# Loading the stacks of q and k for one group at a time, instead of for two

## The chip, the core and the metric

The kernel runs on one core of one Trainium2 chip. The metric is the device time of one execution in microseconds (us). The core has five engines with a queue of instructions each: PE (TensorE, matmuls), DVE (VectorE), ACT (ScalarE), POOL (GpSimd) and SP (SyncE, which here only issues DMA transfers and waits). All DMA transfers share 16 DMA engines. The engines meet only through semaphores.

## The reference

Two layers over x of shape (4, 512, 512). Only the first one has to do with the change. With `xn = layernorm(x)` it is

```python
q = rope((xn @ wq).reshape(4, 512, 32, 16))      # 32 heads of 16
k = rope((xn @ wk).reshape(4, 512, 8, 16))       # 8 heads of 16, each for 4 heads of q
v = (xn @ wv).reshape(4, 512, 8, 16)
...
attn = softmax(q @ k.T / 4 + causal mask)
s = (attn @ v) @ wo
logits = xn @ W_gate + b_gate                    # top 2 of 8 experts for each token
y = relu(xn @ W_e[e] + b_e[e]), mean over the 2 experts of the token
x = x + s * silu(y)
```

The second layer is a long convolution of the layer norm of x, times the silu of a linear layer.

## The kernel before

There are three stages. Stage A (to about 100 us) projects x to q, k, v and gate logits and turns q and k. They are written to DRAM, as two fp32r parts each (a high part and the rest), in `qk_d`, which the profile calls `turned_parts`. Stage B (about 100 to 580 us) is attention and the expert layer, woven into each other. Stage C is the second layer.

**Groups.** Stage B walks over 32 groups, 4 batches `b` times 8 heads of k, `h`; here a group's number is g = 8b + h. A group is the 4 heads of q that share one head of k. Each of its two halves (`s`) has on the partitions a stack of three pieces of 16 rows, (high, low), (high, high), (low, high), so that one matmul over 48 rows gives the product of q and k in nearly full precision. The stack of k is `kt`, that of q is `qt`. Both have four buffers, `[h // 2 % 2, h % 2]`: group g + 4 takes the buffers of group g.

**The two products.** For each group PE makes the scores twice: `scores_1` (10 pieces, L1601), from which DVE takes the maxima (L1399), and `scores_2` (10 pieces, L1627 and L1630), in which two more rows of `qt` bring in the negative maxima and which ACT exponentiates (L1522). The maxima are turned by PE (`turn_maxima`, L1640), rounded by DVE into `m_rows` (L1416, L1418), and put under `qt` by two small transfers, one issued by SP and one by ACT (`maximum_rows`, L1320). Then `values` (L1657) multiplies with v.

**The order on PE in iteration g**, with expert or output matmuls ("quarters" of a tile, L1685 and L1696) between the parts by the table `SIZES`:

```python
scores(e, (3, 4, 5, 6), following, (0, 1, 2, 3), (b, h))
quarters(b, h, 0)
scores(e, (7, 8, 9), following, (4, 5, 6), (b, h))
quarters(b, h, 1, 0, TURN_AFTER)
turn_maxima(e, *following)
quarters(b, h, 1, TURN_AFTER)
scores(e, (0, 1, 2), after, (7, 8, 9), (b, h))
```

The first tuple is of `scores_1`, of `following` (g + 1) or `after` (g + 2); the second is of `scores_2` of g itself. So iteration g needs the stack of g + 2 right behind `turn_maxima`, and is done with the stack of g itself a little later, at the end of the last line.

The number of quarters differs from group to group. From the `turn_maxima` of iteration g to the next there are mostly 8, but 5 for g = 5, 9, 13, 17, 21 and 25, then 7 for g = 6, 10, 14, 18, 22 and 28, and 6 for g = 26 and 27. A quarter is one matmul of 128 x 512 for a tile, which the profile counts as two rows.

**The queue of SP in iteration g** (`go` of `sp_b`) is written in this order: transfers for the expert tiles (`shuffles(b, h, 0)`: L1776 loads the rows of a tile into `xg`, named `arena` in the profile, L1779 stores gathered rows to `gathered_rows`), the maxima of g + 1 (L1320), stores of expert results (L1785), the stacks (odd g only: `load_stacks` for g + 3 and g + 4, L1313 for `kt` and L1314 for `qt`), more tiles (`shuffles(b, h, 1)`), stores, and a few weights. DVE turns a loaded tile (`expert_x`, L1464) before PE can multiply it. SP, DVE and PE all take their instructions strictly in order.

`load_stacks` waits on `b_s2`, the count of pieces of `scores_2`, until the two groups that hold the pair of buffers are through: for g + 3 and g + 4 that is the end of `scores_2` of g. Stacks 0 to 3 are loaded ahead of the loop, and the q and k of group 0 once more, earlier, by `load_first` into `qt_first`.

Of the kernel before, what the change touches and what calls it, by code (L numbers as in the profile page):

```python
# [33 lines left out]
R = H // KV  # L34
# [130 lines left out]
def due(n):  # L165


    return not isinstance(n, int) or n > 0
# [49 lines left out]
def build(nc, x_d, wq_d, wk_d, wv_d, wo_d, wg_d, bg_d, we_d, be_d, lam_d, p_d, q_d, vct_d, ct_d, bp_d, dd_d,  # L218
          step_d, wft_d, sc_d, bf_d, const_d, dft_d, out_d):
    ctx = ExitStack()  # L220
    with ctx:
# [9 lines left out]
        def sems(name, n):  # L231
            return [sem(f"{name}{i}") for i in range(n)]
# [200 lines left out]
        def sp_a(e):  # L433
# [22 lines left out]
            for b in range(NB):  # L456
                for u in range(TPB):
# [2 lines left out]
                        store_parts(e, b - 1, u - 2)  # L460
                    if (b, u) == (NB - 2, 0):
                        load_first(e)
            load_stacks(e, 0, 0)

        def dve_a(e, st):
            v = nc.vector
# [766 lines left out]

        b_init = sem("b_init")
        b_first = sem("b_first")
        b_ld = sems("b_ld", 2)
        b_wo = sem("b_wo")
        b_v = sem("b_v")
        b_tm, b_me, b_mr = sem("b_tm"), sem("b_me"), sem("b_mr")
# [19 lines left out]
        def nth_of(per, b, h, k):  # L1259

            return b * (NG * per) + (h * per + k)
# [26 lines left out]
                    e.dma_start(kt[at:at + HD, 0].bitcast(F32), k_rows[of_k]).then_inc(b_first, 16)  # L1288
                    e.dma_start(qt_first[at:at + HD].bitcast(F32).rearrange("i r t -> i (r t)"), q_rows[of_q, s]).then_inc(b_first, 16)

        def load_stacks(e, b, h):

            e.wait_ge(b_init, 4)
            for half in range(2):
                e.wait_ge(a_ps[half], 16 * (b + 1))
            if due(at := nth_of(NJ, b, h, -2 * NJ)):
                e.wait_ge(b_s2, at)
            if not due(b) and h == 0:
                for par in range(2):
                    e.wait_ge(a_xn[par], NT // 2)  # L1300
            if not due(b) and h == 2:
                for u in (2, 3):
                    e.wait_ge(a_store[u], 16 * NB)
                for par in range(2):
                    e.wait_ge(a_kvg[par], NT // 2)
            buf = h // 2 % 2
            q_rows = qk_d[b][:, R * HD * h:R * HD * (h + 2), :].rearrange("c (g s i r) t -> c s i g (r t)", g=2, s=2, r=HALF)
            k_rows = qk_d[b][:, D + HD * h:D + HD * (h + 2), :].rearrange("c (g i) t -> c i g t", g=2)
            for s in range(2):
                for piece, (of_q, of_k) in enumerate(((0, 0), (0, 1), (1, 0))):  # L1310
                    at = 64 * s + HD * piece
                    if (b, h) != (0, 0):
                        e.dma_start(kt[at:at + HD, buf].bitcast(F32), k_rows[of_k]).then_inc(b_ld[buf], 16)  # L1313
                    e.dma_start(qt[at:at + HD, buf].bitcast(F32).rearrange("i g r t -> i g (r t)"), q_rows[of_q, s]).then_inc(b_ld[buf], 16)  # L1314

        def maximum_rows(e, b, h, s):

# [261 lines left out]
        def scores_1(e, b, h, n):  # L1579
# [4 lines left out]
            if n == 0 and alone_in_bank:  # L1584
                e.wait_ge(b_first, 16 * NLD)
            elif n == 0:
                buf = h // 2 % 2
                e.wait_ge(b_ld[buf], b * (2 * 16 * NLD) + 16 * NLD * (h // 4 + 1) - (16 * NLD // 2 if buf == 0 else 0))
            if n == 2 and b == 0 and h in (1, 2):
                e.wait_ge(b_me, h)  # L1590
            if (b, h) == (0, 1) and n == 0:
# [175 lines left out]
        def sp_b(e):  # L1767
# [19 lines left out]
            def go(b):  # L1787
                for h in range(NG):
                    shuffles(b, h, 0)
                    if b * NG + h + 1 < NB * NG:  # L1790
                        maximum_rows(e, *next_group(b, h, 1), 0)
                    stores(b, h, 0, 1)
                    if h % 2 and b * NG + h + 3 < NB * NG:
                        load_stacks(e, *next_group(b, h, 3))
                    shuffles(b, h, 1)
                    stores(b, h, 2, 3)
                    transform(b, h)
                    if (b, h) in STORES:
                        store_parts(e, NB - 1, STORES.index((b, h)))
                    if (b, h) in WEIGHTS:  # L1800
                        out_weights(WEIGHTS.index((b, h)))
# [26 lines left out]
                e.wait_ge(a_kvg[par], NT // 2)  # L1828
            for x in (E - 2, E - 1):
                load_expert(e, x)  # L1830
            load_stacks(e, 0, 2)
            for b in range(NB):
                go(b)

# [421 lines left out]
```

## Time and profile before

| | us |
|---|---|
| median of 3 runs | 687.88 (686.79 to 691.36) |
| the profiled execution | 685.05 |
| its span, first to last instruction | 683.3 |
| PE busy in it | 617.3 |
| DVE busy in it | 551.2 |

The span is 1.75 us shorter than the time of the same execution. The profiled execution is 2.83 us below the median of the runs.

### The profile page before, as it was taken

The page shows a single profiled execution, that of the slowest core. Times are in us where ns is not written, and L with a number is a line of the kernel's source. Part 1 is how long each engine was busy: PE and PEld are TensorE (multiplying, and loading weights), DVE is VectorE, ACT ScalarE, POOL GpSimd, SP SyncE. Part 2 cuts the span into 40 slices and gives each one's busy share as a digit, 9 for nine tenths or more (in the row PEclk, how much of TensorE's full clock was granted, in tenths as well). Part 3 has the DMA queues.
Part 4 walks back from the last instruction along what each step waited for, and adds up shares of the span by engine and source line. Part 5 has one row for each costly group of instructions (what it writes and reads, how often), then busy time and mean ns, then how long its engine had stood idle before and what let it go on. Part 6 is the DMA issues. An engine that isn't in the chain of part 4 may idle for free.

```text
span 683.3 us, 12195 instructions
## 1 busy us (share of the span) xinstructions
PE 617.3 (90%) x3541; PEld 351.0 (51%) x3565; DVE 551.2 (81%) x1789; ACT 285.4 (42%) x535; POOL 239.5 (35%) x364
## 2 busy tenths in 40 slices
PE   9899998988997999799799889979989899899997
PEld 5788784434443444344344434434434443378886
DVE  6698899869987679788778868977888885869995
ACT  4353325424343335334344433434444445334442
POOL 3777541423232213223221322322123113676630
PEclk9999999979998999999999989999999999999999
DMA  8599978789789365575735647584464816768841
GB/s 271 145 327 246 337 215 170 164 143 295 129 268 213 93 114 101 142 146 158 179 92 105 101 125 146 162 190 88 93 130 121 203 63 216 176 142 209 205 121 77
DMA packets 79903, 113.10 MB, mean 166 GB/s; under 512 B 9705, under 2 KB 42665, under 8 KB 79841
## 3 DMA queue, kind: packets, MB, share of 16 engines
q1 hardware_dynamic: 68098, 86.90, 50.4%
q0 software_dynamic: 6704, 18.62, 12.7%
q10 hardware_dynamic: 5038, 6.84, 4.2%
q8 instruction: 29, 0.48, 0.3%
q14 instruction: 34, 0.27, 0.2%
HBM read 72.15 MB, written 39.65 MB: 164 GB/s over the span
## 4 chain that ended last, share of the span: by engine, by line
PE 52%; DVE 16%; DMA 13%; SPq 8%; issue 5%; POOL 2%; ACT 2%; ACTq 2%; DVEq 0%; POOLq 0%
PE bank L1685 16%; PE bank L1657 8%; DMA qt<-turned_parts 7%; DVE bank L1399 6%; PE bank L2173 6%; PE bank L1601 6%; PE bank L1696 4%; PE bank L2178 4%; PE bank L1026 3%; DMA turned_parts<-qk_parts 3%; SPq L1313 3%; SPq L1314 3%; DMA w_e<-expert_rows,slots 3%; PE bank L1627 1%; DVE m_rows L1418 1%
## 5 line engine op out<-in xcount | busy, mean ns | idle before, releaser
L1399 DVE CUSTOM_DVE_ANT_0 bank<-bank,cst 128x384 f32<-128x384 f32 (+3 forms) x512 | 234.3, 523 | 68.8 <-PE bank L1601 66.6
L1522 ACT ACTIVATE arena<-bank 128x512 f32<-128x512 f32 x320 | 169.6, 601 | 181.1 <-PE bank L1627 128.2
L1337 POOL TENSOR_SCALAR_AFFINE_SELECT arena<-arena 128x512 f32<-128x512 f32 x128 | 80.8, 644 | 329.2 <-ACT arena L1522 329.2
L1685 PE MATMUL bank<-w_e,arena 128*128 x312 | 156.8, 628 | 5.3 <-issue 4.0
L1601 PE MATMUL bank<-kt,qt 48*128 48x512 f32 (+1 forms) x496 | 110.9, 340 | 33.0 <-DMA qt<-turned_parts 20.6
L1601 PEld LDWEIGHTS bank<-kt,qt 48*128 48x128 f32 x496 | 68.9, 189 | 100.9 <-DVE arena L1399 43.8
L1627 PE MATMUL bank<-qt,kt 50*128 50x512 f32 x256 | 95.1, 455 | 0.4 <-ACT arena L1522 0.4
L1685 PEld LDWEIGHTS bank<-w_e,arena 128*128 128x128 f32 x312 | 57.6, 198 | 52.1 <-issue 48.0
L1657 PE MATMUL bank<-arena 128*32 128x512 f32 (+3 forms) x1024 | 78.7, 445 | 0.0
L1399 DVE DVE_READ_ACCUMULATOR2_ANT arena<- 128x1 f32 x512 | 72.0, 141 | 0.0
L1696 PE MATMUL bank<-w_proj,arena 128*128 128x512 f32 x128 | 67.7, 654 | 0.8 <-ACT s_tok L1513 0.8
L1657 PEld LDWEIGHTS bank<-arena 128*32 128x32 f32 x1024 | 28.4, 111 | 55.3 <-issue 46.9
L1532 ACT ACTIVATE arena<-bank 128x512 f32<-128x512 f32 x39 | 23.4, 599 | 63.0 <-PE bank L1685 62.9
L1627 PEld LDWEIGHTS bank<-qt,kt 50*128 50x128 f32 x256 | 45.1, 188 | 4.2 <-ACT arena L1522 3.3
L1026 PE MATMUL bank<-proj_high,xh 128*128 128x264 f32 (+1 forms) x128 | 46.1, 360 | 0.4 <-DVE xl L526 0.4
L1026 PE MATMUL bank<-proj_low,xh 128*128 128x264 f32 (+1 forms) x128 | 43.4, 339 | 0.0
L1026 PE MATMUL bank<-proj_high,xl 128*128 128x264 f32 (+1 forms) x128 | 43.4, 339 | 0.0
L858 POOL TENSOR_TENSOR s_tok<-arena 128x256 f32<-128x256 f32 (+1 forms) x64 | 33.6, 558 | 26.1 <-DVE arena L545 20.4
L1349 POOL DMA_INDIRECT s_tok<-xn_rows,slots_i x39 | 38.8, 994 | 10.9 <-ACT arena L1522 3.8
L1696 PEld LDWEIGHTS bank<-w_proj,arena 128*128 128x128 f32 x128 | 23.0, 199 | 25.8 <-issue 21.6
L541 DVE TENSOR_TENSOR arena<-bank,cst 128x128 f32<-128x128 f32 (+1 forms) x63 | 27.1, 475 | 5.4 <-PE bank L1026 5.1
L1923 POOL DMA_INDIRECT w_e<-expert_rows,slots x16 | 27.2, 1701 | 11.3 <-DMA w_e<-expert_rows,slots 8.1
(168 smaller groups left out, 942.8 us busy)
## 6 DMA issues: line engine op xcount, KB each, us to landing
qt<-turned_parts SPq DMA_DIRECT2D x96, 128.0 KB, 5.7
turned_parts<-qk_parts SPq DMA_DIRECT2D x8, 1280.0 KB, 8.3
gathered_rows<-s_tok SPq DMA_DIRECT2D x39, 256.0 KB, 5.2
arena<-gathered_rows SPq DMA_DIRECT2D x39, 256.0 KB, 4.4
expert_rows<-arena SPq DMA_DIRECT2D x39, 256.0 KB, 2.5
w_e<-in_L_ffn_W_e ACTq DMA_DIRECT2D x24, 256.0 KB, 6.0
kt<-turned_parts SPq DMA_DIRECT2D x96, 64.0 KB, 5.4
arena<-in_L_attn_x SPq DMA_DIRECT2D x16, 256.0 KB, 6.8
```

The lines of the kernel that those rows point to most:

```text
L858: i = g.tensor_tensor(o[:, :, :, c, :], xc[:, :, :, c, :], xs[:, :, :, 1 - c, :], op)
L1026: i = t.matmul(out[u % 2][:, 0:n], x[:, u % 2, k, :], w[part][:, k, :], start=(k == 0 and x is xh and part == 0), stop=(k == KB - 1 and pa ...
L1337: g.affine_select(out=diag, in_=diag, compare_op=ALU.is_ge, fill=0.0, base=0, pattern=[[0, 2], [0, HALF], [1, P]], channel_multiplier=-1). ...
L1349: e.indirect_dma_start(xr[m % 3], None, xn_d, bass.IndirectOffsetOnAxis(ap=slots_i[:, m:m + 1], axis=0)).then_inc(m_x[m % 3], 16)
L1399: i = v.tensor_tensor_reduce(out=part, in0=part, in1=const("mask")[:, S - w:], scale=1.0, scalar=LOWEST, op0=ALU.add, op1=ALU.max, accum_o ...
L1522: nc.scalar.activation(pt[:, s, first:second + 1:second - first].rearrange("p c r q -> p c (r q)"), s2_bank(b, h, n).rearrange("p (c x) -> ...
L1601: i = t.matmul(s1_bank(b, h, n)[:, at:at + w], stack[rows, x if r is None else r, q * P:w], kt[rows, h // 2 % 2, h % 2, 0:w], start=(x == ...
L1627: i = t.matmul(to, keys(j), queries[:, q:q + 2], start=True, stop=True)
L1657: i = nc.tensor.matmul(bank[4][VW * r:VW * (r + 1), j * P:], vb[:, j, h, :], pt[:, r // HALF, at:at + TPB - j, r % HALF, :], start=(j == O ...
L1685: i = t.matmul(bank[7], xgt[:, m % 2, k * P:(k + 1) * P], w_e[:, ex[m], k, :], start=False, stop=(k == KB - 1))
L1696: i = t.matmul(bank[to], ot[:, (b * PAIRS + k) % (PAIRS + 1), u, :], wo[:, k, :], start=(k == 0), stop=(k == KB - 1))
L2173: i = t.matmul(bank[2 + u % 2][:, :], x[:, u % 2, k, :], (w_high, w_low)[part][:, k, :], start=(k + n == 0), stop=(k + n == KB + 1))
```

## The change

The stacks are loaded by `load_stack`, for one group, in twelve transfers of 16 rows (six of `kt`, 32 KB each, six of `qt`, 64 KB each). Before they were twelve for two groups, of 64 and 128 KB. The load of group g + 4 is issued in every iteration g, behind `shuffles(b, h, 1)`, and waits for the end of `scores_2` of g. There are four semaphores `b_ld` in place of two. Bytes and buffers are the same.

```diff
-        def load_stacks(e, b, h):
+        def load_stack(e, b, h):
...
-            if due(at := nth_of(NJ, b, h, -2 * NJ)):
+            if due(at := nth_of(NJ, b, h, -3 * NJ)):
                 e.wait_ge(b_s2, at)
...
-            buf = h // 2 % 2
-            q_rows = qk_d[b][:, R * HD * h:R * HD * (h + 2), :].rearrange("c (g s i r) t -> c s i g (r t)", g=2, s=2, r=HALF)
-            k_rows = qk_d[b][:, D + HD * h:D + HD * (h + 2), :].rearrange("c (g i) t -> c i g t", g=2)
+            keys, queries, loaded = kt[:, h // 2 % 2, h % 2], qt[:, h // 2 % 2, h % 2], b_ld[h % 4]
+            k_rows = qk_d[b][:, D + HD * h:D + HD * (h + 1), :]
+            q_rows = qk_d[b][:, R * HD * h:R * HD * (h + 1), :].rearrange("c (s i r) t -> c s i (r t)", s=2, r=HALF)
             for s in range(2):
                 for piece, (of_q, of_k) in enumerate(((0, 0), (0, 1), (1, 0))):
                     at = 64 * s + HD * piece
-                    if (b, h) != (0, 0):
-                        e.dma_start(kt[at:at + HD, buf].bitcast(F32), k_rows[of_k]).then_inc(b_ld[buf], 16)
-                    e.dma_start(qt[at:at + HD, buf].bitcast(F32).rearrange("i g r t -> i g (r t)"), q_rows[of_q, s]).then_inc(b_ld[buf], 16)
+                    if b or h > 1:
+                        e.dma_start(keys[at:at + HD].bitcast(F32), k_rows[of_k]).then_inc(loaded, 16)
+                    e.dma_start(queries[at:at + HD].bitcast(F32).rearrange("i r t -> i (r t)"), q_rows[of_q, s]).then_inc(loaded, 16)
...
             elif n == 0:
-                buf = h // 2 % 2
-                e.wait_ge(b_ld[buf], b * (2 * 16 * NLD) + 16 * NLD * (h // 4 + 1) - (16 * NLD // 2 if buf == 0 else 0))
+                e.wait_ge(b_ld[h % 4], 16 * NLD * (2 * b + h // 4 + 1) - (16 * NLD // 2 if h % 4 < 2 else 0))
...
                     stores(b, h, 0, 1)
-                    if h % 2 and b * NG + h + 3 < NB * NG:
-                        load_stacks(e, *next_group(b, h, 3))
                     shuffles(b, h, 1)
+                    if b * NG + h + 4 < NB * NG:
+                        load_stack(e, *next_group(b, h, 4))
                     stores(b, h, 2, 3)
```

Ahead of the loop, `load_stacks(e, 0, 0)` and `load_stacks(e, 0, 2)` become two calls of `load_stack` each.

The queue of SP in iteration 6, before, from the maxima of group 7 to those of group 8 ("..." stands for more rows of the same two kinds):

```order
L1320 DMA qt<-m_rows 2x8x128 [waits b_me]
L1785 DMA expert_rows<-arena 128x512 [waits m_ye]
L1779 DMA gathered_rows<-s_tok 128x4x128 [waits m_x1]
L1823 DMA w_proj<-in_L_attn_wo 16x4x512 x2
L1776 DMA arena<-gathered_rows 128x512 [waits m_xt,m_xs0]
L1320 DMA qt<-m_rows 2x8x128 [waits b_me]
```

The same iteration with the change:

```order
L1321 DMA qt<-m_rows 2x8x128 [waits b_me]
L1785 DMA expert_rows<-arena 128x512 [waits m_ye]
L1779 DMA gathered_rows<-s_tok 128x4x128 [waits m_x1]
L1314 DMA kt<-turned_parts 16x512 [waits a_ps1,b_s2,a_ps0,b_init]
L1315 DMA qt<-turned_parts 16x1024
...
L1823 DMA w_proj<-in_L_attn_wo 16x4x512 x2
L1776 DMA arena<-gathered_rows 128x512 [waits m_xt,m_xs0]
L1321 DMA qt<-m_rows 2x8x128 [waits b_me]
```

The load of stack 10 now stands in iteration 6, behind the tile transfer L1779 and ahead of L1823 and L1776; before, iteration 6 had no load.

The queue of SP in iteration 0, before, from the maxima of group 1 to those of group 2:

```order
L1320 DMA qt<-m_rows 2x8x128 [waits b_me]
L1779 DMA gathered_rows<-s_tok 128x4x128 [waits m_x0]
L1779 DMA gathered_rows<-s_tok 128x4x128 [waits m_x1]
L1776 DMA arena<-gathered_rows 128x512 [waits m_xs0]
L1776 DMA arena<-gathered_rows 128x512 [waits m_be,m_xs1]
L1779 DMA gathered_rows<-s_tok 128x4x128 [waits m_x2]
L1320 DMA qt<-m_rows 2x8x128 [waits b_me]
```

With the change:

```order
L1321 DMA qt<-m_rows 2x8x128 [waits b_me]
L1779 DMA gathered_rows<-s_tok 128x4x128 [waits m_x0]
L1779 DMA gathered_rows<-s_tok 128x4x128 [waits m_x1]
L1314 DMA kt<-turned_parts 16x512 [waits a_ps1,b_s2,a_ps0,b_init]
L1315 DMA qt<-turned_parts 16x1024
...
L1776 DMA arena<-gathered_rows 128x512 [waits m_xs0]
L1776 DMA arena<-gathered_rows 128x512 [waits m_be,m_xs1]
L1779 DMA gathered_rows<-s_tok 128x4x128 [waits m_x2]
L1321 DMA qt<-m_rows 2x8x128 [waits b_me]
```

The load of stack 4 moved ahead of the first two tile loads (L1776); before, stacks 4 and 5 were loaded in iteration 1, behind the second L1320.

## Rows read from the trace of the kernel before

**Rows 1.** The page, busy time: engine, us, share of the span, instructions.
```profile
PE 617.3 (90%) x3541; PEld 351.0 (51%) x3565; DVE 551.2 (81%) x1789; ACT 285.4 (42%) x535; POOL 239.5 (35%) x364
...
```

**Rows 2.** The page, the chain that ended last, by line.
```profile
PE bank L1685 16%; PE bank L1657 8%; DMA qt<-turned_parts 7%; DVE bank L1399 6%; PE bank L2173 6%; PE bank L1601 6%; PE bank L1696 4%; PE bank L2178 4%; PE bank L1026 3%; DMA turned_parts<-qk_parts 3%; SPq L1313 3%; SPq L1314 3%; DMA w_e<-expert_rows,slots 3%; PE bank L1627 1%; DVE m_rows L1418 1%
```

**Rows 3.** Waits of PE: total us, times, longest us.
```profile
PE bank L1601 <- DMA qt<-turned_parts: 20.6, 8, 4.1
```

**Rows 4.** Timeline, PE: start, us, what, [idle before it <-releaser].
```profile
217.83 0.79 PE L1601 MATMUL bank<-kt,qt 48*128 48x512 f32 x1 [3.82 <-DMA qt<-turned_parts]
...
511.85 0.50 PE L1601 MATMUL bank<-kt,qt 48*128 48x512 f32 x1 [2.17 <-DMA qt<-turned_parts]
...
537.86 0.49 PE L1601 MATMUL bank<-kt,qt 48*128 48x512 f32 x1 [1.28 <-DMA qt<-turned_parts]
```

**Rows 5.** Windows from one L1640 of PE to the next: engines, PEclk, DMA share, GB/s.
```profile
202.21:213.68 11.47, 10.72 (x73) 5.03 (x72) 10.91 (x42) 6.05 (x12) 4.63 (x6) 1.00 0.79 138
213.68:233.43 19.75, 15.45 (x76) 7.11 (x78) 11.86 (x44) 6.18 (x12) 2.51 (x4) 0.83 0.58 144
274.03:291.42 17.39, 14.04 (x75) 6.31 (x77) 12.47 (x45) 6.17 (x12) 4.58 (x6) 0.90 0.51 133
331.71:350.43 18.72, 14.15 (x76) 6.71 (x78) 12.79 (x51) 6.17 (x12) 2.51 (x4) 0.91 0.43 112
391.03:410.54 19.51, 15.59 (x76) 7.03 (x78) 12.46 (x45) 6.17 (x12) 4.57 (x6) 0.83 0.49 121
451.40:468.76 17.36, 14.18 (x77) 6.37 (x78) 11.86 (x44) 6.19 (x12) 2.51 (x4) 0.90 0.42 129
509.35:523.87 14.52, 11.72 (x74) 5.55 (x75) 11.75 (x48) 6.16 (x12) 4.41 (x6) 1.00 0.59 170
523.87:536.26 12.39, 11.64 (x74) 5.53 (x75) 11.73 (x49) 6.16 (x12) 3.46 (x5) 1.00 0.71 125
536.26:550.54 14.28, 12.52 (x76) 6.15 (x78) 12.32 (x50) 6.18 (x12) 2.51 (x4) 1.00 0.47 163
550.54:564.79 14.25, 13.32 (x79) 6.30 (x79) 11.79 (x45) 6.20 (x12) 2.51 (x4) 1.00 0.22 76
```

**Rows 6.** Timeline, SP, DMA issues from 203 to 215 us.
```profile
203.22 0.62 SPq L1320 DMA_DIRECT2D qt<-m_rows  x1
...
204.45 0.49 SPq L1313 DMA_DIRECT2D kt<-turned_parts  x1
...
210.27 0.42 SPq L1314 DMA_DIRECT2D qt<-turned_parts  x1
...
213.19 0.42 SPq L1779 DMA_DIRECT2D gathered_rows<-s_tok  x1
214.85 0.62 SPq L1320 DMA_DIRECT2D qt<-m_rows  x1
```

**Rows 7.** The chain in order of time: start, us, what.
```profile
210.27 7.52 DMA qt<-turned_parts
```

**Rows 8.** Timeline, PE, first second-scores of the group after 203 us.
```profile
206.66 0.73 PE L1627 MATMUL bank<-qt,kt 50*128 50x512 f32 x2
```

**Rows 9.** Timeline, SP, around the first group of the loop.
```profile
130.53 1.23 SPq L1779 DMA_DIRECT2D gathered_rows<-s_tok  x2
133.19 1.20 SPq L1776 DMA_DIRECT2D arena<-gathered_rows  x2
```

**Rows 10.** Timeline, DVE, the first expert tile turned.
```profile
140.32 0.70 DVE L1464 STREAM_TRANSPOSE arena<-arena 128x512 f32<-128x512 f32 x1
```

**Rows 11.** Windows: four iterations; a stretch with a pair of stacks loaded; one without.
```profile
202.21:262.56 60.35, 52.95 (x303) 24.47 (x305) 47.19 (x176) 24.62 (x47) 13.72 (x20) 0.94 0.60 124
234.44:249.60 15.16, 13.57 (x79) 6.12 (x78) 12.20 (x43) 6.20 (x12) 4.07 (x6) 1.00 0.92 165
249.60:263.57 13.97, 13.21 (x83) 6.45 (x83) 12.22 (x49) 6.43 (x13) 2.51 (x4) 1.00 0.13 42
```

More of the change, by code:

```diff
@@ L462, in sp_a @@
                         load_first(e)
-            load_stacks(e, 0, 0)
+            for h in (0, 1):
+                load_stack(e, 0, h)
         def dve_a(e, st):
@@ L1235, in build @@
         b_first = sem("b_first")
-        b_ld = sems("b_ld", 2)
+        b_ld = sems("b_ld", 4)
         b_wo = sem("b_wo")
@@ L1830, in sp_b @@
                 load_expert(e, x)
-            load_stacks(e, 0, 2)
+            for h in (2, 3):
+                load_stack(e, 0, h)
             for b in range(NB):
```

## The prediction

> **What bounds the kernel now.** I read the busy times first: PE is busy for 90% of the span, DVE for 81% [rows 1]. So time can be won on PE's path, if DVE leaves room. The chain that ended last is next: it is PE for the most part, but 7% of the span, some 48 us, stands under a transfer, `qt<-turned_parts`, the stack of q [rows 2]. A chain counts a transfer from its issue, so that is no measure of what PE lost. The list of waits is: PE sat idle for 20.6 us in 8 waits in front of L1601, `scores_1`, for that transfer [rows 3]. The timeline shows them in front of the first piece of `scores_1` of g + 2, right behind `turn_maxima`: 3.82 us at 217.83, 2.17 at 511.85, 1.28 at 537.86 [rows 4]. Seven of the eight are longer than 1 us; they lie in iterations 6, 10, 14, 18, 22, 26 and 28.
>
> Why there: in iteration 5 SP issued the maxima at 203.22, then the twelve transfers of stacks 8 and 9 from 204.45 to 210.7 [rows 6]; the last landed 7.52 us after its issue at 210.27, at 217.8 [rows 7]. PE wanted stack 8 at 214.0, when `turn_maxima` of iteration 6 was through. The turns at 202.21 and 213.68 are only 11.47 us apart, since 5 quarters lie between them, against 14.25 us for 8 [rows 5]. A pair needs about 13.4 us from first issue to landing, and has some 9.6 there. In the other odd iterations there are 7 or 8 quarters, and the load makes it.
>
> A stall costs more than its idle time. The windows from turn to turn show the granted clock: 1.00 in the undisturbed ones, 0.83, 0.90, 0.91, 0.83 and 0.90 in the five with the longest stalls, so that for a part of them PE ran at the lower of its two levels, 1.2 GHz, after it had stood still [rows 5].
>
> **What the change removes.** Stack g + 4 is loaded in iteration g and needed in iteration g + 2, behind the turn. Take stack 8. It is issued in iteration 4, when PE's `scores_2` of group 4 is through, about one group ahead of 203 us, and is needed at 214: over 20 us for half of the bytes, where the pair took 13.4 us. So all seven waits should go. The price of each is the window with the stall less what the same number of quarters takes without it:
>
> - 7 quarters without a stall: the window from 536.26 is 14.28 us at clock 1.00 and holds the 1.28 us stall, so 13.00. As a check, 8 quarters take 14.25, and a quarter less, at some 0.95 us, gives 13.3; 6 quarters take 12.39 [rows 4, 5].
> - The five windows at a reduced clock: 19.75 + 17.39 + 18.72 + 19.51 + 17.36 = 92.73, less 5 x 13.00 = 65.00, is 27.7 us.
> - From 509.35 (6 quarters): 14.52 - 12.39 = 2.1 us. From 536.26: 1.3 us.
>
> Together **31.1 us**. By the idle time alone it would be 20.6 [rows 3]; the other 10.5 is the clock.
>
> DVE has room, but little. In the stalled windows it was busy for 11.9 to 12.8 us, and 13.0 are left to it; from 523.87 it was busy for 11.73 of 12.39 us [rows 5]. Two windows, with 12.8 and 12.5, may end some tenths late. I take 0.8 us off, between nothing and 3 (five windows at the 95% of rows 5 give 12.8 / 0.95 = 13.5 at the worst, 0.5 more each).
>
> **What it adds.** SP issues 186 more transfers (6 for stacks 0 and 1, 180 for stacks 2 to 31), at 0.47 us from one to the next [rows 6]: 87 us, 5.6 per group. Odd iterations have had a load of twelve already. The new ones stand in the even iterations. Behind them on SP wait the tile loads (L1776) of the next iteration and the next maxima.
>
> - The maxima. SP has to be free when DVE has rounded them. In iteration 5 it was free at 213.6, and the maxima went out at 214.85; that iteration keeps twelve issues and loses half of the bytes [rows 6]. An even iteration of SP lasts from one turn to the next, 12.4 us or more (6 quarters, g = 26), for 5.6 us of load and some 3 of tiles. From the issue at 203.22 PE had 3.44 us until it wanted them, at 206.66, and no wait is shown there [rows 6, 8]. I cost this at nothing; the cover is that 1.2 us of SP. If it is gone, each us late is a us of PE.
> - The tile loads. They are placed a group or so ahead of the DVE turn of that tile, and 5.6 us of lateness is less than that. Nothing, with one exception.
> - The exception is iteration 0. Stack 4 goes ahead of the first two tile loads. These went out at 133.19; with twelve issues from 131.8 on they go out at about 137.4 [rows 9]. DVE turned the first tile at 140.32 [rows 10], and PE's first expert matmul waits for that. A landing 4 to 5 us after the issue comes at 141.5 to 142.5, that is 1.2 to 2.2 us behind DVE's turn. I take 1.5 us; the ends are 0 and 4.
> - The DMA engines move the same bytes. With a pair loaded in it a window showed a share of 0.92, without one 0.13 [rows 11]; now both get a half. That can only smooth it, so nothing, unless a smaller transfer is dearer (below). For smoothing and for SP late here or there I take 0.3 us off.
>
> Of pages of the Trainium skill one speaks against this edit: "DMA: Bandwidth & Descriptors", section Bandwidth, asks for transfers of 1 MiB and calls those under 64 KB dominated by their descriptors, and the pieces of k go from 64 to 32 KB. No row here has a 32 KB piece of a stack, so the trace neither agrees nor differs; if it held in full here, the third rival would be the outcome.
>
> **The sum.** 31.1 - 0.8 - 1.5 - 0.3 = 28.5 us. The profiled execution, 685.05, would become 656.5 (span 654.8), and the median, 2.83 above it, **659.4 us**, 4.1% less.
>
> **The rivals.**
>
> 1. *PE catches up, but the next thing is late.* Behind a stall DVE and ACT had time to get ahead; without it PE meets DVE's maxima, which it already does at L1640. Then only the idle time comes back, 20.6 us less 2.6 as above, 18.0, and 670 us. Against it: windows with DVE busy for 95% exist [rows 5]. Chance 0.09.
> 2. *The stall stays.* The load now stands behind `shuffles(b, h, 1)`, which waits for tiles to be turned. If that held it back by 10 us, stack 8 would still be in time, since it has over 20. I give 0.02; the time would be the old one, about 687.
> 3. *Halved transfers cost the DMA engines as much as whole ones.* A pair costs them 0.92 x 15.16 - 0.13 x 13.97 = 12.1 us at full share, tiles included. Two pairs in four iterations at twice that are 24 us on top of the 0.60 x 60.35 = 36.2 that those have now, 60.4 in all, where four iterations would take 60.35 - 6.75 = 53.6 [rows 5, 11]. Then the DMA engines would bound the loop at its present pace, so 685 to 690 us. For it: the share is above 0.9 while a pair loads. Against it: a piece has the same rows of 4 KB and 2 KB. Chance 0.04.
> 4. *Slower: the tile loads come late.* In 15 even iterations of the loop L1776 stands behind 5.6 us of new issues. If DVE waited for the tile in its strict order, maxima and PE would wait behind it. It decides against the change from 31.1 / 15 = 2.1 us a time; with nothing of the 5.6 hidden it is 15 x 5.6 - 31.1 = 53 us more, 741; with half of it, 11 us more, 699. Against it: no DVE row of before waits for a tile at L1464, with stack loads twice as long ahead of half of them. Chance 0.03.
>
> **How the numbers follow.** The forecast gets 0.82. Its bounds: no loss and a few tenths of smoothing give 31.5 less, 656.4, or 655.3 from the lowest run of before (686.79); a loss of 4 at the start and 3 from DVE gives 664. The range goes on to rival 1; with the scatter of a median it is 654 to 670.5. A measurement of this kernel can tell about 1%, 7 us. Faster by over 1%: 0.92 (the forecast, rival 1, a small rest). Within 1%: 0.05 (rivals 2 and 3). Slower: 0.03.
>
> **What would show it.** In the changed profile PE should have no wait above 0.5 us in front of L1601 for `qt<-turned_parts`, and the chain no share of it. From the turn of iteration 6 to the next it should be 13.0 to 13.5 us at a granted clock of 1.00. SP should show 180 issues of `kt` in `load_stack` and 192 of `qt`, 0.47 us apart, with the maxima (L1320, now L1321) still going out within 0.1 us of DVE's L1418. DVE should wait 1 to 2 us at the first L1464, near 140 us, and nowhere else for a tile. I am wrong if a DVE row waits for `gathered_rows` in many groups (rival 4), if the DMA share stays near 1 throughout (rival 3), or if the seven windows keep 15 us or more at clock 1.00 (rival 1).

## The result and the profile after

The changed kernel takes 653.92 us (median of 4 runs, 653.36 to 656.67), where the kernel before took 687.34 (4 runs, 682.38 to 691.36). The ratio is 0.9525, with a 95% interval of 0.9456 to 0.9594: faster by 4.7%. The profiled execution took 656.67 us, with a span of 654.9, the highest of the four. It was beside 685.05 for the profiled execution of before, so from profile to profile the change is 28.4 us.

First the page of the changed kernel: the busy times, the queue that SP feeds (packets, MB, the packets' time as a share of 16 engines' span), the chain by line and the issues of q.

```profile
PE 605.2 (92%) x3541; PEld 348.9 (53%) x3565; DVE 549.0 (84%) x1789; ACT 285.9 (44%) x535; POOL 238.3 (36%) x364
...
q1 hardware_dynamic: 71074, 86.91, 44.8%
...
PE bank L1685 17%; DVE bank L1400 10%; PE bank L1027 8%; PE bank L1657 8%; PE bank L1601 7%; PE bank L2174 7%; PE bank L1696 5%; PE bank L2179 4%; DMA w_e<-expert_rows,slots 3%; PE bank L1627 2%; PE bank L1004 1%; DVE arena L1400 1%; ACTq L1321 1%; DVE arena L1465 1%; PE bank L2163 1%
...
qt<-turned_parts SPq DMA_DIRECT2D x192, 64.0 KB, 2.7
```

PE's busy time fell by 12 us, from 617.3 to 605.2, with the same work [rows 1]. That fits the clock, since the matmuls are the same. The chain has lost its share for the stack of q, `DMA qt<-turned_parts` [rows 2]. The last row is the edit itself: 192 transfers of 64 KB, landing 2.7 us after the issue (median), where 96 of 128 KB took 5.7.

Then the waits, which are engine and line, what they waited for, total us, times, longest us. The first fence is PE's list, the second DVE's.

```profile
PE bank L1601 <- DVE arena L1400: 13.0, 31, 1.2
PE bank L1640 <- DVE arena L1409: 7.0, 13, 2.6
...
PE bank L1685 <- DVE arena L1465: 3.8, 2, 2.9
```

```profile
DVE arena L1465 <- DMA arena<-gathered_rows: 2.9, 1, 2.9
```

PE has no wait left at L1601 for a stack [rows 3]. What stands at the head now is DVE, in many waits of 0.4 us each. DVE waits once for an expert tile, 2.9 us, which it never did before.

Windows of the changed kernel from one L1640 of PE to the next, as in [rows 5]. The first is the short one of iteration 5; the seven behind it are those in which the old kernel stalled.

```profile
201.63:213.12 11.49, 10.73 (x73) 5.03 (x72) 10.91 (x42) 6.05 (x12) 4.61 (x6) 1.00 0.83 235
213.12:226.05 12.93, 12.45 (x77) 6.15 (x78) 11.75 (x44) 6.18 (x12) 2.50 (x4) 1.00 0.71 187
266.65:279.48 12.83, 12.35 (x76) 6.08 (x77) 12.36 (x45) 6.16 (x12) 4.39 (x6) 1.00 0.53 140
319.77:332.82 13.05, 12.48 (x77) 6.17 (x78) 12.58 (x51) 6.17 (x12) 2.50 (x4) 1.00 0.57 166
373.40:386.21 12.81, 12.33 (x75) 6.09 (x77) 12.34 (x45) 6.17 (x12) 4.40 (x6) 1.00 0.53 142
427.09:440.03 12.94, 12.46 (x77) 6.16 (x79) 11.74 (x44) 6.17 (x12) 2.50 (x4) 1.00 0.42 125
480.61:492.88 12.27, 11.63 (x74) 5.53 (x75) 11.82 (x48) 6.17 (x12) 4.39 (x6) 1.00 0.74 176
505.27:518.21 12.94, 12.46 (x76) 6.15 (x78) 12.20 (x50) 6.18 (x12) 2.50 (x4) 1.00 0.36 119
```

All seven are at clock 1.00. They sum to 89.77 us, against 121.53 for the same seven before. The window from 213.12, once 19.75 us, is 12.93 now.

SP's timeline in iteration 4 shows why. Stack 8 goes out there, twelve issues, some 17 us ahead of the turn at 213.12.

```profile
190.80 0.33 SPq L1314 DMA_DIRECT2D kt<-turned_parts  x1
...
195.82 0.48 SPq L1315 DMA_DIRECT2D qt<-turned_parts  x1
```

The two spans can be laid side by side, cut at the same turns of PE. The sums are differences of turn times:

| stretch | before | after | change |
|---|---|---|---|
| to the turn in iteration 0 | 128.84 | 126.36 | -2.5 |
| from there to the turn in iteration 4 | 58.70 | 61.02 | +2.3 |
| from there to the turn in iteration 6 | 26.14 | 25.74 | -0.4 |
| the seven windows that had a stall | 121.53 | 89.77 | -31.8 |
| the rest of the loop | 229.58 | 229.58 | 0.0 |
| behind the last turn | 118.51 | 122.43 | +3.9 |
| span | 683.3 | 654.9 | -28.4 |

Two rows of it can't be put down to the edit. In the stretch to the turn in iteration 0 the new kernel is ahead by 2.44 us already when it issues its first changed transfer (93.59 us, in the old one 96.03). The stretch behind the last turn took 121.7 us in another execution of the old kernel (below), so 3.2 of its 3.9 us lie within the scatter of the old kernel.

The 2.3 us in the second row come from the edit, as the third experiment shows. They are in SP's and DVE's timeline at the start of the loop:

```profile
129.35 0.46 SPq L1314 DMA_DIRECT2D kt<-turned_parts  x1
...
134.97 0.42 SPq L1315 DMA_DIRECT2D qt<-turned_parts  x1
135.44 0.90 SPq L1776 DMA_DIRECT2D arena<-gathered_rows  x2
...
137.96 0.62 SPq L1321 DMA_DIRECT2D qt<-m_rows  x1
```

```profile
140.85 0.71 DVE L1465 STREAM_TRANSPOSE arena<-arena 128x512 f32<-128x512 f32 x1 [2.92 <-DMA arena<-gathered_rows]
```

The tile loads (L1776) go out at 135.44, behind the twelve issues of stack 4, not at 133.19 [rows 9]. DVE waits 2.92 us for the tile. PE's window behind it, 21.01 us in place of 17.69, lost the idle and some clock (0.74, before 0.82).

### The profile page after: what moved, and what is told of

Same layout as the page of the kernel before. It is cut to its first block, busy times and chain, and to the rows that moved or that the text cites. A ratio compares the mean times of both kernels' runs of the same rounds, so it can differ in the third digit from the quotient of the medians.

```text
span 654.9 us, 12411 instructions
## 1 busy us (share of the span) xinstructions
PE 605.2 (92%) x3541; PEld 348.9 (53%) x3565; DVE 549.0 (84%) x1789; ACT 285.9 (44%) x535; POOL 238.3 (36%) x364
## 3 DMA queue, kind: packets, MB, share of 16 engines
q1 hardware_dynamic: 71074, 86.91, 44.8%
## 4 chain that ended last, share of the span: by engine, by line
PE 64%; DVE 20%; DMA 4%; issue 4%; POOL 2%; SPq 2%; ACT 2%; ACTq 1%; DVEq 0%; POOLq 0%
PE bank L1685 17%; DVE bank L1400 10%; PE bank L1027 8%; PE bank L1657 8%; PE bank L1601 7%; PE bank L2174 7%; PE bank L1696 5%; PE bank L2179 4%; DMA w_e<-expert_rows,slots 3%; PE bank L1627 2%; PE bank L1004 1%; DVE arena L1400 1%; ACTq L1321 1%; DVE arena L1465 1%; PE bank L2163 1%
## 5 line engine op out<-in xcount | busy, mean ns | idle before, releaser
L1685 PE MATMUL bank<-w_e,arena 128*128 x312 | 151.1, 609 | 7.5 <-DVE arena L1465 3.8
L1601 PE MATMUL bank<-kt,qt 48*128 48x512 f32 (+1 forms) x496 | 108.3, 336 | 13.1 <-DVE arena L1400 13.0
L1601 PEld LDWEIGHTS bank<-kt,qt 48*128 48x128 f32 x496 | 67.7, 187 | 80.2 <-DVE arena L1400 44.3
L1627 PE MATMUL bank<-qt,kt 50*128 50x512 f32 x256 | 93.7, 449 | 0.8 <-ACT arena L1523 0.4
L1685 PEld LDWEIGHTS bank<-w_e,arena 128*128 128x128 f32 x312 | 55.9, 192 | 52.0 <-issue 48.2
L1696 PE MATMUL bank<-w_proj,arena 128*128 128x512 f32 x128 | 64.6, 629 | 0.8 <-ACT s_tok L1514 0.8
L1657 PEld LDWEIGHTS bank<-arena 128*32 128x32 f32 x1024 | 28.5, 110 | 50.5 <-issue 42.3
L1627 PEld LDWEIGHTS bank<-qt,kt 50*128 50x128 f32 x256 | 44.4, 186 | 4.7 <-ACT arena L1523 3.3
L1696 PEld LDWEIGHTS bank<-w_proj,arena 128*128 128x128 f32 x128 | 22.5, 195 | 24.7 <-issue 20.5
L1924 POOL DMA_INDIRECT w_e<-expert_rows,slots x16 | 27.4, 1710 | 13.7 <-DMA w_e<-expert_rows,slots 10.5
```

Of the source, the lines that this page charges most:

```text
L1601: i = t.matmul(s1_bank(b, h, n)[:, at:at + w], stack[rows, x if r is None else r, q * P:w], kt[rows, h // 2 % 2, h % 2, 0:w], start=(x == ...
L1627: i = t.matmul(to, keys(j), queries[:, q:q + 2], start=True, stop=True)
L1657: i = nc.tensor.matmul(bank[4][VW * r:VW * (r + 1), j * P:], vb[:, j, h, :], pt[:, r // HALF, at:at + TPB - j, r % HALF, :], start=(j == O ...
L1685: i = t.matmul(bank[7], xgt[:, m % 2, k * P:(k + 1) * P], w_e[:, ex[m], k, :], start=False, stop=(k == KB - 1))
L1696: i = t.matmul(bank[to], ot[:, (b * PAIRS + k) % (PAIRS + 1), u, :], wo[:, k, :], start=(k == 0), stop=(k == KB - 1))
```

## The experiments

Ten runs, the first four on one chip and the other six on another. Edits are against the changed kernel, save where it says otherwise. Each ratio is to the old kernel, run on the same chip.

### One iteration less in hand

The change does two things at once: it halves what must land before the first of the two groups can start, and it issues that stack an iteration earlier. Here stack g + 3 is loaded in iteration g, as late as the old kernel had it, but by itself.

```diff
-                    if b * NG + h + 4 < NB * NG:
-                        load_stack(e, *next_group(b, h, 4))
+                    if 0 < b * NG + h and b * NG + h + 3 < NB * NG:
+                        load_stack(e, *next_group(b, h, 3))
```

> The changed kernel, but in iteration g stack g + 3 is loaded, not g + 4: one stack in twelve transfers, yet at the time at which the old kernel began its pair, so with only one iteration in hand. It tells the earlier issue from the smaller load. Theory (the old kernel was late because the first stack was counted as landed only with the second): twelve transfers from 204.4 to 210 us, landing some 3 us later at 213, just ahead of 214.0, where PE wants the stack. Waits in front of L1601 for the stack below 1 us each, windows behind the turns of iterations 6, 10, 14, 18 and 22 of 13 to 14 us at clock 1.00, time within 1% of the changed kernel, 652 to 659. Rival (the second iteration in hand is what helped, since transfers queue behind others on the way): waits of 1 to 3 us come back in the five or seven places, with part of the clock loss, 662 to 675.

Measured: 654.84 us (650.85 to 656.41), ratio 0.9499 (0.9452 to 0.9546), where the changed kernel had 0.9525. The two times can't be set against each other as they are, since this edit also takes the load out of iteration 0: its stretch from the turn of iteration 0 to that of iteration 4 is 57.05 us, not 61.02. The seven windows can be: they sum to 89.72 us, against 89.77. Its windows around iteration 6, and its issues of stack 8:

```profile
197.90:209.39 11.49, 10.88 (x73) 5.01 (x72) 10.92 (x42) 6.06 (x12) 4.61 (x6) 1.00 0.81 236
209.39:222.34 12.95, 12.62 (x77) 6.15 (x78) 11.74 (x44) 6.17 (x12) 2.50 (x4) 1.00 0.76 188
```

```profile
200.44 0.33 SPq L1314 DMA_DIRECT2D kt<-turned_parts  x1
...
205.53 0.42 SPq L1315 DMA_DIRECT2D qt<-turned_parts  x1
```

The last of the twelve goes out at 205.53, and the turn that needs them is at 209.39, only 3.9 us later. PE still doesn't wait for the stack. In the old kernel the last of the twelve went out 8.1 us behind the turn of iteration 5, here 7.6 us behind it, so what changed is the landing: the old one took 7.52 us [rows 7], this one some 4 at most. So the earlier issue is not what wins; half of the bytes behind the same twelve issues is enough.

### Pairs again, of single loads

Here the single loads are made two at a time, in every odd iteration and at the old place ahead of `shuffles(b, h, 1)`: 24 issues in a row.

```diff
+                    if h % 2 and b * NG + h + 3 < NB * NG:
+                        for n in (3, 4):
+                            load_stack(e, *next_group(b, h, n))
                     shuffles(b, h, 1)
-                    if b * NG + h + 4 < NB * NG:
-                        load_stack(e, *next_group(b, h, 4))
```

> The changed kernel's single loads and semaphores, but both issued in odd iterations, at the place of the old pair: stack g + 3, then g + 4, 24 transfers in a row. Theory (SP's queue has 1.2 us to spare in iteration 5, and the maxima pay for what is more): the first stack lands in time as in the run before, but SP is busy until about 216 and then has the tiles of iteration 6 to do, so that the maxima of group 7, rounded at 214.8, go out at 218 to 219 in place of 214.85; PE wants them at about 217.5, and waits 2 to 4 us in front of L1627 in the five places behind the short iterations. 662 to 675 us. Rival (what hurt was only that one semaphore stood for two stacks, and SP's time is free): the time of the changed kernel, 652 to 657.

Measured: 687.26 us (682.1 to 696.62, 10 runs), ratio 0.9969 (0.9939 to 0.9998). All of the gain is gone, where the theory had 662 to 675 us. The profiled execution took 695.0, some 8 us above the median. PE's list of waits says where to look:

```profile
PE bank L1627 <- DMA qt<-m_rows: 20.6, 8, 4.5
```

Eight waits and 20.6 us as in the old kernel, but at another line and for another transfer: L1627 is the first matmul of `scores_2`, and `m_rows` are the maxima that SP moves. SP's queue in iteration 5, and PE behind it:

```profile
203.49 0.48 SPq L1314 DMA_DIRECT2D kt<-turned_parts  x1
...
214.73 1.89 SPq L1315 DMA_DIRECT2D qt<-turned_parts  x1
...
218.14 0.84 SPq L1776 DMA_DIRECT2D arena<-gathered_rows  x2
219.03 0.42 SPq L1779 DMA_DIRECT2D gathered_rows<-s_tok  x1
219.50 0.62 SPq L1321 DMA_DIRECT2D qt<-m_rows  x1
```

```profile
223.10 0.51 PE L1627 MATMUL bank<-qt,kt 50*128 50x512 f32 x2 [4.38 <-DMA qt<-m_rows]
```

The first stack was there in time: PE has no wait for one at L1601. The second twelve kept SP until 216.6, and with what stands between, the maxima of the next group went out at 219.50, 6.8 us behind the turn. In the changed kernel they go out 1.2 us behind it, at 214.29. PE stood still for 4.38 us. The tile load went out late as well, at 218.14, and DVE waited 4.84 us for it; over the run it has six such waits, 12.7 us in all. The seven windows are 20.47, 17.58, 18.44, 17.61, 16.62, 19.58 and 17.19 us long, a stall's length again. The prediction had costed the maxima at nothing, covered by 1.2 us of SP; this run made the maxima 5.6 us late, and 4.38 of that reached PE, so the cover is real and about that small. It is why one stack per iteration works, and not two in a row.

### The first tiles ahead of the load

The one loss that the prediction named, at the start of the loop, is taken away: stack 4 is loaded in iteration 1, not 0.

```diff
+                    if (b, h) == (0, 1):
+                        load_stack(e, 0, 4)
                     shuffles(b, h, 1)
-                    if b * NG + h + 4 < NB * NG:
+                    if 0 < b * NG + h and b * NG + h + 4 < NB * NG:
```

> The changed kernel, but stack 4 is loaded in iteration 1, behind the maxima of group 2, and so behind the first two tile loads; nothing else moves. Theory (the one place where the change costs something is iteration 0): the wait of DVE of 2.9 us at the first L1465 is gone, the stretch from the turn of iteration 0 (126.36 us in the changed profile) to that of iteration 4 (187.38) shrinks from 61.0 to about 58.7 us, as in the old kernel, and the time falls by 2 us, 652. Rival (the wait only replaces a slower clock or a wait of DVE for PE that comes behind it): no change within 0.2%.

Measured: 653.35 us (651.19 to 655.88), ratio 0.9491 (0.9456 to 0.9526). DVE no longer waits for a tile. From the turn of iteration 0 to that of iteration 4 it is 58.32 us, against 61.02, and the window of the first tile is

```profile
138.20:155.50 17.30, 16.70 (x79) 7.31 (x80) 10.50 (x41) 6.05 (x12) 4.39 (x6) 0.82 0.58 159
```

with 17.30 us, where the changed kernel has 21.01 and the old one 17.69. So the delayed tile loads cost 2.7 us of span here. On this chip the changed kernel itself did not run, so the medians are compared below.

### The old kernel, with PE kept busy in the stall

This is the old kernel. In the five iterations with the longest stalls PE runs twelve matmuls on ones, whose result nobody reads, ahead of the scores that wait for the stack.

```diff
                     quarters(b, h, 1, TURN_AFTER)
+                    if b * NG + h in (6, 10, 14, 18, 22):
+                        e.wait_ge(b_m, nth_of(NJ, *after, -2))
+                        keep_awake(12, s1_bank(*after, 0))
                     scores(e, (0, 1, 2), after, (7, 8, 9), (b, h))
```

> The old kernel with its pairs, where in iterations 6, 10, 14, 18 and 22 PE runs 12 matmuls on constants ahead of the waiting scores_1, into the bank that scores_1 then overwrites. They take 2.6 us of the wait of 2.7 to 4.1 us and change no result. It tells the idle time from the clock. Theory (of the 31 us 20.6 is idle time and 10.5 is the lower clock behind it): the stack still lands at the same time, but the granted clock is 1.00 in the five windows, which take 13.0 plus the stall, 15.9 to 17.1 us, in place of 17.4 to 19.8: 10 us less than the old kernel, a ratio of 0.984 to 0.988. Rival (the clock falls for another reason, or the slower work behind the stall was hidden): a ratio of 0.997 to 1.003 and clock 0.83 to 0.91 still.

Measured: 677.0 us (673.93 to 680.64), ratio 0.9848 (0.9808 to 0.9889). The five windows of this kernel, and PE in the first of them:

```profile
211.49:228.49 17.00, 15.94 (x90) 7.58 (x91) 11.99 (x44) 6.17 (x12) 2.50 (x4) 1.00 0.64 167
269.08:284.97 15.89, 15.15 (x88) 7.13 (x89) 12.47 (x45) 6.17 (x12) 4.57 (x6) 1.00 0.57 147
325.27:341.11 15.84, 15.27 (x89) 7.23 (x90) 12.79 (x51) 6.17 (x12) 2.50 (x4) 1.00 0.44 129
381.73:398.02 16.29, 15.16 (x88) 7.16 (x89) 12.46 (x45) 6.16 (x12) 4.57 (x6) 1.00 0.56 144
440.18:455.70 15.52, 15.20 (x89) 7.23 (x90) 11.87 (x44) 6.17 (x12) 2.50 (x4) 1.00 0.47 140
```

```profile
211.66 2.75 PE L982 MATMUL bank<-ones_b 128*128 128x512 bf16 x12
215.40 0.49 PE L1601 MATMUL bank<-kt,qt 48*128 48x512 f32 x1 [0.99 <-DMA qt<-turned_parts]
```

The stack comes no earlier: PE is through with the twelve matmuls at 214.4 and waits another 0.99 us. But the clock is 1.00 in all five. Together they are 15.5 us above 5 x 13.00, about the length of the five dummy runs (2.75 us each) and the waits behind them. In the old kernel's profile it was 27.7, of which 16.9 were the five waits for a stack (3.82, 2.86, 4.08, 3.44 and 2.71), so 10.8 was clock. The medians, 688.03 for the old kernel (17 runs on this chip) and 677.0, differ by 11.0 us, with bounds of 7.6 and 13.2 from the interval. So the clock share is shown by medians too, since the matmuls bring no stack sooner.

### Smaller pieces

Two kernels ask whether small transfers are dear. In the first every transfer of a stack is cut in two, 24 to a stack; in the second only those of q, 18 to a stack. The semaphore's thresholds follow.

```diff
-                    e.dma_start(queries[at:at + HD].bitcast(F32).rearrange("i r t -> i (r t)"), q_rows[of_q, s]).then_inc(loaded, 16)
+                    for part in range(2):
+                        both = slice(S * part, S * (part + 1))
+                        e.dma_start(queries[at:at + HD, part].bitcast(F32), q_rows[of_q, s][:, both]).then_inc(loaded, 16)
```

> The changed kernel, each transfer of a stack cut into two of half the size (16 KB of k, 32 KB of q): 24 in a row for each stack, the same bytes. Theory (it is SP's queue that is short, 0.47 us a transfer, not the DMA engines): a load holds SP for 11.2 us, an iteration of SP needs about 14.4 us with maxima, tiles and stores, while PE's iterations are 13.4 us on average and 11.5 at the shortest. The maxima go out late in nearly every iteration, PE waits at L1627 for them, most behind the short ones, and the loop runs at the pace of SP, 31 x 14.4 = 446 in place of 406 us: 685 to 705 us, no wait for the stacks at L1601. Rival (SP waits for most of its time and has room): 652 to 662 us.

> The changed kernel with only the transfers of q cut into two (32 KB each): 18 in a row for each stack. A dose between the changed kernel and the run with 24, and small pieces without a full queue. Theory (SP): a load holds SP for 8.4 us, an iteration needs 11.6, less than the average of 13.4 us; behind the short iterations, of 11.5 us, the maxima go out 1 to 2 us late, which the 3.4 us until PE wants them still covers for the most part. Waits for the maxima at L1627 of 1 us at most each, 653 to 660 us. Rival (small pieces cost the DMA engines more): the share of q1 in the list of queues rises from 44.8% by a fifth or more, stacks and tiles land later, 660 us or more, without late maxima on SP.

Measured: with 24 transfers 724.0 us (717.97 to 726.98), ratio 1.0548 (1.049 to 1.0606); with 18 transfers 671.19 (668.47 to 673.18), ratio 0.9767 (0.9708 to 0.9825). The changed kernel took 660.9 on the same chip, so six more issues to a stack cost 10.3 us and twelve more 63. First the waits of PE and of DVE with 24:

```profile
PE bank L1629 <- DMA qt<-m_rows: 31.6, 14, 4.6
```

```profile
DVE arena L1467 <- DMA arena<-gathered_rows: 23.2, 9, 6.8
```

Lines stand two higher here: L1629 is L1627, L1603 is L1601, L1467 is L1465. PE waits 14 times for maxima, and DVE nine times for tiles: the mechanism of rival 4, which 11 us of issues per iteration bring on and 5.6 don't, but for the first tile. The theory had 685 to 705 us, from late maxima alone. With 18:

```profile
PE bank L1629 <- DMA qt<-m_rows: 4.7, 3, 3.5
...
PE bank L1603 <- DMA qt<-turned_parts: 2.8, 1, 2.8
```

```profile
95.31 14.06 SPq L1317 DMA_DIRECT2D qt<-turned_parts  x24
109.42 1.45 SPq L1323 DMA_DIRECT2D qt<-m_rows  x2
```

There are three late maxima and one late stack. That one is ahead of the loop: 24 issues of q, 14 us, keep the maxima of group 0 back till 109.42, and the first turn of the loop comes at 132.69, 5.2 us later than in the changed kernel on this chip (127.50). In the loop a wait for maxima is long only once, 3.55 us at 217.90, and that window, from the turn of iteration 5, takes 16.85 us in place of 11.48. The start, from iteration 0 to 4, is 1.8 us longer. In no other window does the kernel lose to the changed one, so the loss lies in three places and is not a price for every group. Both expectations missed the time: the theory had 653 to 660 us, and the rival's sign, a share of q1 that rises, did not come.

Do the DMA engines pay for the small pieces? The page gives, for the queue that SP feeds, packets, MB and the packets' time as a share of 16 engines' span. Here the old, the changed kernel, 24 and 18 transfers, in this order; the changed kernel's row stands in the first fence.

```profile
q1 hardware_dynamic: 68098, 86.90, 50.4%
```

```profile
q1 hardware_dynamic: 82978, 86.93, 41.2%
```

```profile
q1 hardware_dynamic: 77218, 86.92, 44.7%
```

Share times span is 50.4% x 683.3 = 344 us before, 44.8% x 654.9 = 293 after, 41.2% x 716.2 = 295 with 24 transfers and 44.7% x 668.1 = 299 with 18. The run with pairs of single loads, 24 in a row, has 42.1% x 693.3 = 292. So a half-size piece took less of the engines' time, not more, whether spread over iterations or in a row, and a quarter size piece took no more than half size. The halving made no more packets of data either: by the pages of the profile, 70198 of 512 B and over before and 70200 after, and the 2975 that were added are smaller ones. Why they took less time is not shown. What small pieces cost is SP: some 0.46 us an issue.

### The old and the changed kernel again

One execution of the old kernel and several of the changed one, on the chip of the small pieces.

> The old kernel once more, for a second profile of it. The waits for the stacks in front of L1601 are the same seven, 20 us plus or minus 2 in all, with the clock below 1.00 in at least four of the windows behind them; the stretch behind the last turn is 118.5 to 123 us (118.5 in the first profile, 121 to 124 in those of the changed kernel and of the three experiments), which would show that its difference has nothing to do with the change. Rival: 118.5 again, within 0.5 us, and then the change has made that stretch longer by some 3 us.

> The changed kernel once more, for a second profile and beside the others on this chip. The wait of DVE at the first L1465 is there again, 2 to 4 us, and the stretch from the turn of iteration 0 to that of iteration 4 is 59 to 61 us. Time 652 to 657 us. If the stretch is 61.0 again the wait costs 2.3 us in each run; if it is 59 or less, the low clock behind it in the first profile was a matter of chance.

Measured: the old kernel 681.45 us, span 679.7; the changed one 660.9 (660.01 to 661.57), ratio 0.9615 (0.9566 to 0.9664). The old kernel's wait for stacks, in this execution:

```profile
PE bank L1601 <- DMA qt<-turned_parts: 15.3, 8, 3.6
```

That is 15.3 us in eight waits, 5 less than in [rows 3]; the seven windows sum to 113.3 us, not 121.5. Three of them show how the clock goes with the wait, which is 3.58 us in the first, 2.22 in the second and 1.72 in the third:

```profile
327.81:346.00 18.19, 14.29 (x77) 6.92 (x78) 12.81 (x51) 6.18 (x12) 2.50 (x4) 0.91 0.41 114
443.43:458.66 15.23, 12.69 (x77) 6.15 (x78) 11.86 (x44) 6.18 (x12) 2.50 (x4) 1.00 0.47 142
499.26:514.96 15.70, 13.51 (x74) 5.83 (x75) 11.75 (x48) 6.15 (x12) 4.39 (x6) 0.89 0.55 154
```

The seven waits are 2.64, 2.26, 3.58, 0.83, 2.22, 1.72 and 1.80 us here. The clock fell behind five of them (0.89 to 0.91) and stayed at 1.00 behind those of 0.83 and 2.22. The seven windows are 113.30 - 90.39 = 22.91 us above undisturbed ones; 15.05 of it is the waits, so 7.9 the clock, where [rows 5] had 10.8. So how much the old kernel loses differs between executions, though the places don't. The expectation, 18 to 22 us of waits, missed. The shortest wait, 0.83, stands behind a short window that was itself long, 13.75 us at clock 0.88 in place of 11.47, so the stack had 2.3 us more to land.

The changed kernel was slower here than in the first measurement, and than the 652 to 657 us expected. In its profiled execution two short windows took 13.95 us each in place of 11.5, at iterations 9 to 10 and 17 to 18. The window of the first of them, whole, and 4.1 us of it:

```profile
255.98:269.93 13.95, 12.40 (x72) 5.28 (x71) 10.51 (x44) 6.04 (x12) 4.44 (x6) 0.88 0.48 138
262.70:266.80 4.10, 4.07 (x9) 1.41 (x9) 2.84 (x13) 1.20 (x3) 0.64 (x1) 0.58 0.90 269
```

```profile
262.73 0.44 PE L1601 MATMUL bank<-kt,qt 48*128 48x384 f32 x1 [1.28 <-DVE arena L1400]
```

```profile
263.23 3.55 PE bank L1696 x4
```

The clock was 0.58 for 4 us, right behind a wait of 1.28 us for DVE. In those 4 us four matmuls of L1696 take 3.55 us. A third profile of the same code (the next section) has such a wait in the same place:

```profile
261.73 0.44 PE L1601 MATMUL bank<-kt,qt 48*128 48x384 f32 x1 [1.33 <-DVE arena L1400]
```

There the clock stayed at 1.00, the four matmuls took 1.98 us and the window 12.37. So of the 2.5 us some 0.9 are DVE being late and 1.6 the clock. The old kernel has such a window on this chip too, the 13.75 us above, so they don't come with the edit alone. Twice 2.5 us would make 5 of the 7 us between the medians of the two measurements, but the third profile, of a median of 659.27, has only twice 0.9, so they don't explain it. DVE's wait at the start was 3.0 us.

### The changed kernel and the first-tiles version side by side

> The changed kernel a third time, as the measure for the run beside it on the same chip. 653 to 661 us; the wait of DVE for the first tile again 2 to 4 us.

> The kernel with the first tiles ahead of stack 4, now on the same chip as the changed kernel. Theory (the wait of 2.9 us ahead of the first tile costs 2 to 2.5 us): 1.5 to 3 us below the changed kernel beside it. Rival: within 1 us of it.

Measured on the same chip, six runs each: the changed kernel 659.27 us (658.7 to 662.81), ratio 0.9643 (0.9588 to 0.9699); with the first tiles ahead of stack 4, 653.98 (653.7 to 657.9), ratio 0.9564 (0.951 to 0.9618). From the turn of iteration 0 to that of iteration 4 it is 60.84 against 57.31 us, so 3.5 of the 5.3 us between the medians lie where the edit is. That is more than the 1.5 to 3 us expected. Of the 5.8 us between the two profiled spans another 2.7 lie behind the last turn (123.69 against 120.98), and that stretch scatters from 118.5 to 123.7 us over the twelve profiles, those of the old kernel among them. So the gap of the medians is not all the edit's. For the start itself all profiles can be used: the stretch from iteration 0 to 4 takes 60.6 to 61.0 us in the three of the changed kernel, and 56.6 to 58.8 in the seven that load nothing in iteration 0, the old kernel's three among them (58.70, 58.78 and, with the dummy matmuls, 56.58). The means are 60.8 and 57.8, so the load there costs some 3 us. On both chips the median of this version is the lowest of those measured there.

## Why the prediction was right

**The bound and the mechanism** held. The stalls in front of L1601 were a pair that needs 13.4 us in 9.6. They went, in the seven iterations named, and nothing took their place: rivals 1 and 2 fell with the windows at 12.27 to 13.05 us and clock 1.00. What the prediction offered as the reason, 20 us in hand for stack 8, was more than is needed. Loaded an iteration later a stack lands too.

**The main term**, 31.1 us: the seven windows gave 31.8. The five stalled ones were to fall to 13.00 each; they fell to 12.93, 12.83, 13.05, 12.81 and 12.94. The split into 20.6 idle and 10.5 clock stood on window lengths alone; the twelve dummy matmuls bear it out, with 11.0 us by the medians (7.6 to 13.2). It isn't a constant, though: the second execution of the old kernel had 7.9.

**DVE's 0.8 us** did not come. DVE was busy for 11.7 to 12.6 us in these windows, and the longest, 13.05, is that with 12.58. The 0.3 for smoothing is not seen either: the rest of the loop has 229.58 us in both profiles.

**The start** is the term that was mis-sized. The prediction took 1.5 us between 0 and 4. DVE's wait was 2.9, 3.0 and 2.7 in three executions, and the stretch from iteration 0 to 4 lost 2.7 us against the first run without the early load, 3.5 against the one beside it, some 3 by the means. Counted from the turn of iteration 0, the tile loads were to go out 8.6 us later (137.4 in the old trace's time) and went out 9.1 us later (135.44); they landed 5.4 us behind that, at 140.8, where 4 to 5 were supposed; and DVE was ready when the old trace said, 11.5 to 11.6 us behind the turn (137.9 here). So the wait of 2.9 in place of 1.5 us is 0.5 of SP and 0.9 of the landing. And an idle at the start costs clock too: 0.74 in the window for 0.82.

**The maxima** at nothing: right for twelve issues, with no wait above 0.3 us in this profile and none above 1.0 in the kernel's two others. With 24 in a row, or with 18 or 24 to a stack, the cover of 1.2 us is gone and PE waits at L1627, as the step said it would.

**Rival 3** fell: the packets' time went from 344 to 293 us when pieces were halved. The page "DMA: Bandwidth & Descriptors" of the Trainium skill, section Bandwidth, has transfers under 64 KB dominated by their descriptors. Here the pieces of k went from 64 to 32 KB and the engines' time didn't rise, so this case gives no support to it as a reason against the edit.

**Rival 4** is a real mechanism at twice the issues: 24 transfers to a stack gave 724.0 us and nine waits for tiles, 24 in a row in every second iteration gave six. At twelve it happens once, at the first tile.

**The number.** Profile to profile 28.5 us were forecast and 28.4 came, but in part by luck: gains of 31.8 in the windows, 2.5 ahead of the loop and 0.4 between, less 2.3 at the start and 3.9 behind the loop. The median, 653.92, lies 5.5 us below the forecast and a hair under the range's low end of 654.0. The prediction carried the old kernel's 2.83 us between profiled execution and median over to the new one; there the profiled execution was the highest of four, 2.75 above the median. Measured twice more, on the chip of the last six runs, the medians were 660.9 and 659.27, where the forecast was. Why the same kernel differs by 5 to 7 us between measurements stays open.

## What to carry to other kernels

Price a stall by the window between two fixed points, less the same window undisturbed, not by the idle time: here up to 10.8 of 27.7 us was the clock behind the idle. When a load is late, ask first how much has to land before the first user can start; cutting the load at that border was enough here, and issuing it earlier as well added nothing to the seven windows. Then count the issues, for a queue that works in order: at 0.46 us apiece, twelve more in a row lost the whole gain, by holding back small transfers that somebody waits for, and six more to a stack cost 10 us, in three places where the queue had no room.

## What had not been expected of the hardware

- An issue from SP mostly took 0.42 us, 0.46 to 0.47 from one to the next, for 32 and 64 KB [the issues of stack 8 above], and the same for 64 and 128 KB [rows 6].
- The same bytes in half-size pieces took the packets of SP's queue 15% less time (344 to 293 us), with as many packets of data, and a piece of q landed in 2.7 us, not in 5.7.
- The granted clock fell to 0.58 for 4.1 us behind a wait of only 1.28 us. It did not behind one of 1.33 us in the same place in another execution of the same code. Behind the old kernel's waits for stacks, in two executions, it fell after all eight of 2.26 us and more, and after two of the six between 0.8 and 2.3 us that are shorter (1.72 and 1.80, not 2.22 and 2.17).
